# Turned probabilities kept in landing order, and the row scatters spread out, in a two-layer gated attention and expert kernel

## The reference

```
# cross attention: 16 heads, 8 key/value heads, 128 context tokens of width 128
q = (layernorm(x) @ Wq);  k = ctx @ Wk;  v = ctx @ Wv
attn = softmax(where(mask, q k^T / sqrt(128), -inf))
x = x + tanh(g) * ((attn v) @ Wo)
# 8 experts, each token takes 2; a shared expert beside them
logits = x @ W_router.T;  rw, sel = top_k(softmax(logits), 2)
x = x + tanh(g) * (shared(x) * sigmoid(x @ W_sgate.T) + sum of rw * expert_sel(x))
```

## Time and profile before

| | us |
|---|---|
| median of 3 runs (1302.22 to 1304.45) | 1303.56 |
| the profiled execution | 1302.48 |
| its span in the profile | 1300.7 |
| mean granted clock of TensorE | 0.989 |
| busy: PE, DVE, ACT, POOL | 1240.1, 894.9, 738.5, 549.1 |
| the next stage begins (first product with `ws`) | 1108.56 |

### The profile page before, as it was taken

One profiled execution on the slowest core, in us unless ns is written; L12 is line 12 of the kernel. 1 busy time (PEld: TensorE's weight loads), 2 busy tenths in 40 slices (PEclk: granted clock), 3 DMA queues, 4 the chain that ended last, 5 costly groups with the idle time before them and its releaser, 6 DMA issues. The chain is left out here.

```text
span 1300.7 us, 23370 instructions
## 1 busy us (share of the span) xinstructions
PE 1240.1 (95%) x7907; PEld 1098.9 (84%) x7907; DVE 894.9 (69%) x2453; ACT 738.5 (57%) x2053; POOL 549.1 (42%) x542
## 2 busy tenths in 40 slices
PE   6899999999999989999999989999999988999998
PEld 4788888888888878888888888899988977888987
DVE  6678788887988776743433346657687776788857
ACT  4777787777877743322222247666565653546542
POOL 3564456644565533200000001866668675223430
PEclk9999999999999989999999999999999998999999
DMA  7000000000000310398100011434343355413434
GB/s 266 10 1 1 9 1 1 1 9 0 0 0 1 74 31 2 113 326 245 64 0 1 1 18 49 142 112 136 100 138 130 115 179 166 118 45 99 129 100 174
DMA packets 85672, 101.09 MB, mean 78 GB/s; under 512 B 16985, under 2 KB 72802, under 8 KB 85186
## 3 DMA queue, kind: packets, MB, share of 16 engines
q1 hardware_dynamic: 82162, 90.45, 23.1%
q0 software_dynamic: 3408, 9.34, 2.0%
HBM read 53.60 MB, written 46.18 MB: 77 GB/s over the span
## 5 line engine op out<-in xcount | busy, mean ns | idle before, releaser
L98 PE MATMUL bank<-wvo_hi,pc_hi_a 128*128 128x256 f32 x512 | 149.7, 292 | 6.5 <-DVE pc_lo_a L1337 5.7
L1748 ACT ACTIVATE act_g_f<-bank 128x512 f32<-128x512 f32 x64 | 38.2, 598 | 190.9 <-PE bank L100 190.9
L100 PE MATMUL bank<-wvo_hi,pc_lo_a 128*128 128x256 f32 x512 | 144.8, 283 | 0.0
L99 PE MATMUL bank<-wvo_lo,pc_hi_a 128*128 128x256 f32 x512 | 144.6, 283 | 0.0
L1807 DVE TENSOR_TENSOR hid_f<-act_g_f,bank 128x512 f32<-128x512 f32 x64 | 44.0, 688 | 142.3 <-ACT act_g_f L1748 142.3
L877 ACT ACTIVATE probs_a<-bank,nbias_a,q_r_a 128x128 f32<-128x128 f32 x256 | 114.4, 472 | 23.7 <-DVE nbias_a L995 23.4
L140 POOL TENSOR_TENSOR rstd<-mv,half 128x4 f32<-128x4 f32 x12 | 12.2, 1020 | 260.7 <-DVE mv L135 260.7
L1055 POOL TENSOR_TENSOR probs_a<-probs_a,rden_a 128x512 f32<-128x512 f32 x64 | 66.6, 1041 | 103.8 <-DVE rden_a L1001 103.8
L98 PEld LDWEIGHTS bank<-wvo_hi,pc_hi_a 128*128 128x128 f32 x512 | 98.2, 192 | 12.5 <-DVE pc_lo_a L1337 8.3
L1277 ACT ACTIVATE probs_a<-probs_a,nmin_a 128x128 f32<-128x128 f32 x256 | 99.5, 392 | 7.7 <-DVE nmin_a L1321 7.4
L99 PEld LDWEIGHTS bank<-wvo_lo,pc_hi_a 128*128 128x128 f32 x512 | 98.5, 192 | 3.2
(11 more groups left out here) (314 smaller groups left out, 4139.9 us busy)
## 6 DMA issues: line engine op xcount, KB each, us to landing
rows_in<-blank_f SPq DMA_DIRECT2D x8, 2193.0 KB, 21.1
staged<-blocks_a SPq DMA_DIRECT2D x32, 512.0 KB, 2.9
turned_a<-staged SPq DMA_DIRECT2D x128, 128.0 KB, 2.9
xs_raw_f<-rows_in SPq DMA_DIRECT2D x39, 129.0 KB
y_tok_f<-rows_out SPq DMA_DIRECT2D x4, 1024.0 KB, 8.9
we_raw<-in_L_ffn_We_gate_up SPq DMA_DIRECT2D x2, 1408.0 KB, 9.9
ctx_raw_a<-in_ctx SPq DMA_DIRECT2D x8, 256.0 KB, 3.0
x_sb<-in_x SPq DMA_DIRECT2D x4, 512.0 KB, 10.1
```

Of the source, the lines that this page charges most:

```text
L98: nc.tensor.matmul(out, w[0], x[0], start=start, stop=False)
L99: nc.tensor.matmul(out, w[0], x[1], start=False, stop=False)
L100: return nc.tensor.matmul(out, w[1], x[0], start=False, stop=stop)
```

## The change

Four things, all in the second attention and the router. `pt` keeps the order in which the turned probabilities land (block, head, token); the context product then gives its columns in that order, and `Ch` and `Cl` read the bank and write `pc` through views that put heads and tokens right. A step `SC` issues one scatter, for one slot, so that a group has eight steps: group 0's at s = 35 to 42 (it had four of two scatters at 35 to 38), group 1's at 51, 52, 53 and 58 to 62 (51 to 54). Group 2's routing moves ahead by up to two iterations: NA from s = 52 to 50, the moments and root from 53 to 51, NX from 56 to 54, RT from 57 to 56, RQ from 60 to 58, PL from 63 to 61. The last transpose, unit 63's, moves from the start of v = 64 to the end of v = 63.

```diff
@@ second_order
-               30: "RQ0", 32: "RQ1", 33: "RK0", 34: "PL0 PL1", 35: "SC0", 36: "SC1", 37: "SC2", 38: "SC3"}
-    hurried = {15: "E0", 17: "E1", 20: "NA0 NA1", 21: "NA2 NA3 NM0", 22: "NB0 NB1", 23: "NB2 NB3", 24: "NX0 NX1", 25: "RT0 RL0", 26: "RS0",
-               28: "RQ0", 29: "RQ1", 30: "RK0", 31: "PL0 PL1"}
+               30: "RQ0", 32: "RQ1", 33: "RK0", 34: "PL0 PL1"}
+    scatter = [{35 + n: f"SC{n}" for n in range(8)}, {51: "SC0", 52: "SC1", 53: "SC2", 58: "SC3", 59: "SC4", 60: "SC5", 61: "SC6", 62: "SC7"}]
+    hurried = {15: "E0", 17: "E1", 18: "NA0 NA1", 19: "NA2 NA3 NM0", 20: "NB0 NB1", 21: "NB2 NB3", 22: "NX0 NX1", 24: "RT0 RL0", 25: "RS0",
+               26: "RQ0", 27: "RQ1", 28: "RK0", 29: "PL0 PL1"}
...
-        unit(v - 1, "TV")
+        if v < U:
+            unit(v - 1, "TV")
...
+        for r in range(2):
+            words(scatter[r].get(s, ""), r)
         unit(s, "Ch", "Cl")
...
+        if v == U - 1:
+            unit(v, "TV")
         words(following.get(s, ""))
@@ second_attention
+        def by_block(v):
+            return v.rearrange("p h (i t) -> p i h t", i=4)
...
-                    nc.scalar.activation(flat(pc[0][:, n % 2, :, :]), c_bank[n % 2][:, :], ACT.Copy).then_inc(sem("pc_hi_ready"), 1)
+                    nc.scalar.activation(by_block(pc[0][:, n % 2, :, :]), c_bank[n % 2][:, :].rearrange("p (i h t) -> p i h t", i=4, h=QH), ACT.Copy).then_inc(sem("pc_hi_ready"), 1)
...
-                    hi, lo = (flat(v[:, n % 2, :, :]) for v in pc)
-                    nc.vector.tensor_tensor(lo, c_bank[n % 2][:, :], f32(hi), ALU.subtract).then_inc(sem("pc_ready"), 1)
+                    hi, lo = (by_block(v[:, n % 2, :, :]) for v in pc)
+                    nc.vector.tensor_tensor(lo, c_bank[n % 2][:, :].rearrange("p (i h t) -> p i h t", i=4, h=QH), f32(hi), ALU.subtract).then_inc(sem("pc_ready"), 1)
...
-                    nc.gpsimd.tensor_copy(pt[0][:, n % 2, :].rearrange("p (h i t) -> p i h t", h=QH, i=4),
-                                          turned[:, n // 2 % 2, :, n % 2, :].rearrange("p i (h t) -> p i h t", h=QH)).then_inc(sem("pt_hi_ready"), 1)
+                    nc.gpsimd.tensor_copy(pt[0][:, n % 2, :].rearrange("p (i x) -> p i x", i=4), turned[:, n // 2 % 2, :, n % 2, :]).then_inc(sem("pt_hi_ready"), 1)
...
-                    hi, lo = (v[:, n % 2, :].rearrange("p (h i t) -> p i h t", h=QH, i=4) for v in pt)
-                    nc.gpsimd.tensor_tensor(lo, turned[:, n // 2 % 2, :, n % 2, :].rearrange("p i (h t) -> p i h t", h=QH), f32(hi),
-                                            ALU.subtract).then_inc(sem("pt_ready"), 1)
+                    hi, lo = (v[:, n % 2, :].rearrange("p (i x) -> p i x", i=4) for v in pt)
+                    nc.gpsimd.tensor_tensor(lo, turned[:, n // 2 % 2, :, n % 2, :], f32(hi), ALU.subtract).then_inc(sem("pt_ready"), 1)
@@ Router.gpsimd_step
-            b = m * GB + i
+            b, r = m * GB + i // 2, i % 2
             pool.wait_ge(self.places_ready, m + 1)
-            for r in range(2):
-                self.scatter(self.pay[:, b, :], self.row_of[:, r, b:b + 1], self.rows_in[:, :], self.rows_sent)
+            self.scatter(self.pay[:, b, :], self.row_of[:, r, b:b + 1], self.rows_in[:, :], self.rows_sent)
@@ routed_feed_forward, extras: the same scatters, in the same places, as eight steps a group
-        0: [..., "SC 2 0", "SC 2 1", "SC 2 2", "SC 2 3"],
+        0: [..., *(f"SC 2 {n}" for n in range(8))],
-        7: ["PL 3 0", "PL 3 1", "SC 3 0", "SC 3 1", "SC 3 2", "SC 3 3", "SE 4"],
+        7: ["PL 3 0", "PL 3 1", *(f"SC 3 {n}" for n in range(8)), "SE 4"],
```

More of the change, by code:

```diff
@@ L2136, in routed_feed_forward @@
     extras = {
[1 row of a table removed]
+        0: ["NB 3 0", "NB 3 1", "NB 3 2", "NB 3 3", *(f"SC 2 {n}" for n in range(8))],
         1: ["X 1 0", "X 1 1", "SD 0", "SD 1", "SD 2"],
```

## The result

The changed kernel takes 1292.7 us at the median of 6 runs (1290.94 to 1293.85), the kernel before 1303.46 (1302.22 to 1304.87) in 6 beside them: a ratio of 0.9915, with a 95% interval of 0.9902 to 0.9928. It is faster, by 10.8, which is under 1%. The profiled execution took 1293.64, with a span of 1291.9. Both kernels run 23370 instructions; TensorE is busy for 1238.0 against 1240.1.

What follows compares the result with a forecast made beforehand. TensorE bounds steady slices; elsewhere it waits for GpSimd, slowed by scatter pairs, and VectorE. 1.8 + 8.7 + 1.6 - 1.6 = 10.5, rounded down to 10.2, gave 1292.3 profiled, 1293.4 median; range 1290 to 1299.5.

Steps and rivals of the forecast that it cites:

- Bound and places: Second attention: TensorE sets the pace, falling short where scatters go out, at 999.64 (1.82) and units 54 to 56 (7.2).
- Landing order, nothing: GpSimd's copy and subtraction, context bank readers: simpler or permuted views bring no gain and no loss.
- The slower rival: VectorE's permuted low halves rise by 1.0 to 1.7, making the kernel 8 slower, 1311.6; chance 0.05.
- Group 0, 1.8: Group 0's scatters, s = 35 to 42: one per iteration removes TensorE's wait at 999.64, 1.8 gained.
- (a): Group 2's root at s = 51: GpSimd waits for VectorE's moments, unit 53's copy 2.4 later, TensorE waits 1.3 to 1.4.
- (b): GpSimd's queue up to unit 57's subtraction, fewer scatters ahead: unit 57's context product starts earlier, 5.4 gained.
- the rival of an early fall: Stalls at units 51 to 54 halve TensorE's clock from unit 54; gain only 4.7, 1298.9; chance 0.18.
- (c): Unit 57's product to its low half: ScalarE's context copies are freed of token copies and most router delay, 3.2 gained.
- The tail, nothing: Units 57 to 63, paced by VectorE: 20.0 instead of 21.6, the 1.6 cancelled by 1.6 allowed for half clock.
- The rival in which scatters hold VectorE up by 3.3: Tail: five scatters each delay VectorE by 0.65, 3.3 lost, gain 6.9, 1296.7; chance 0.14.
- The one in which nothing reaches the end: VectorE's fixed queue sets the tail, so only group 0's 1.8 or less is gained, 1301.8; chance 0.06.
- The rule weighed there: VectorE two-input or two-port instructions and GpSimd's exclude each other; earlier trace agreed for copies, showed no wait for scatters.

Runs made afterwards that it cites:

- run 23370: Not a follow-up run: both kernels, the changed one and the one before, run 23370 instructions.
- The second profile: The changed kernel once more, unaltered, profiled a second time and timed in 5 runs: 1291.67 us, ratio 0.9905.

## Why the prediction was right, and where its sizes were off

**Bound and places: held.** Both stretches with a wait for GpSimd's low half were set by pairs of scatters: put the pairs back, and each wait is back (1.89 at unit 40; with the routing late as before, 1.54, 3.29 and 1.51 at units 54 to 56, where the kernel before had 1.58, 3.21 and 2.42).

**Landing order, nothing: held.** Subtraction 1290 ns against a forecast near 1290, low half 690; undone, the same. The slower rival needed a low half of 1.5, and fell.

**Group 0, 1.8: undersized.** It measured 2.4. I priced the wait as it is listed; the product that waits came 2.36 late.

**(a) The root's wait: held.** Counted from unit 50's product (1047.24 in the trace of before, 1046.69 now), I had the moments at 7.8 and unit 53's copy at 10.0; they came at 7.7 and 10.0 (1054.37 and 1056.70). The waits at units 53 and 54 were 1.23 and 0.89, for 1.3 to 1.4 each. What the walk had not asked is what stands behind this wait: VectorE's low half, nearly as late.

**(b) Unit 57's product, 5.4: held.** 32.60 to 27.20 is 5.4; the product was to come 27.16 behind unit 50's, at the full clock that was assumed. The granted clock from 1050 to 1075 shows 1.00, and 0.47 to 0.50 for each product up to unit 57's says the same, so the rival of an early fall did not come.

**(c) The tokens' and router's copies ahead of the low half, 3.2: oversized.** It gave 2.1. The mechanism is there (the low half came 5.01 after its product, not 7.14), but I gave VectorE's sums 0.84 and laid everything end to end; two of their operations alone, on 4 elements each, took 0.48 and 1.08 beside GpSimd's copy and subtraction. The second profile has 4.55 for this stretch (1072.88 to 1077.43), a gain of 2.6, so part of the miss is the spread of a single profile.

**The tail, nothing: the number held, 0.4, and part of that is luck.** I had a stretch shorter by 1.6 and 1.6 of half clock against it. The second profile, at a full clock throughout, needed 19.95 from unit 57's low half to the next stage, which is the 20.0 of the walk: a gain of 1.6. In the first the clock was indeed at half around unit 58 (0.89 over the slice from 1065), but that isn't what ate the gain. With the landing order undone the clock was at half there too (0.66 from 1075 to 1080), and the stretch took 19.96. The 1.2 lay in VectorE's queue, 18.24 against 17.02. And the walk let that queue set the pace to its end, while it does so only to unit 59's low half; behind it TensorE is busy for all of the last 10.74. Nor did I see unit 58's wait of 2.90 for its transfer. The rival in which scatters hold VectorE up by 3.3 falls with the run that took them out: stage 282.54 against 282.25 and 280.62. The one in which nothing reaches the end falls with the stage, 10.4 shorter. The last transpose, costed at nothing, is not settled: 1.4 and 3.0 in the stage, nothing in the median.

**The rule weighed there: it held for copies, and not for scatters.** Small operations of VectorE that start beside a subtraction of GpSimd's end with it. GpSimd's timeline of the changed kernel:

```profile
1077.47 1.27 POOL L1381 TENSOR_TENSOR pt_lo_a<-turned_a,pt_hi_a 128x512 fp32r<-128x512 f32 x1
...
1087.16 1.27 POOL L1381 TENSOR_TENSOR pt_lo_a<-turned_a,pt_hi_a 128x512 fp32r<-128x512 f32 x1
```

and VectorE's, of an operation on 32 elements a partition:

```profile
1087.19 1.27 DVE L2026 TENSOR_SCALAR chosen_r<-rank_r 128x32 f32<-128x32 f32 x1
1088.38 0.17 DVE L2027 TENSOR_SCALAR chosen_r<-rank_r 128x32 f32<-128x32 f32 x1
```

The same kind of operation takes 0.17 right behind; the long one ends at 1088.46, the subtraction at 1088.43. The gates' 1.08 at 1077.69 ends at 1078.77, the subtraction at 1078.74. In the run without scatters in the tail L2026 falls elsewhere and takes 0.17. VectorE's low half, which reads one of its inputs from a bank, is not held up: twelve of them that start beside a subtraction take 0.67 to 0.69, as the others do. That is the rule of the Trainium skill, "SBUF — State Buffer", "Who interferes with whom", by which the later of two such instructions waits; the trace agrees, if VectorE runs these one-input operations in the two-port mode that the rule asks for, which no row shows. Taking the five scatters away shortened nothing, as the trace of before had it.

**The sum.** 2.4 + 5.4 + 2.1 + 0.4 is 10.4 in the stage (10.37 before each term is rounded); 10.5 was forecast, rounded down to 10.2. The two errors in size, 0.6 and -1.1, and the tail's 0.4 nearly cancel. That the match is so close is luck: the second profile has 12.0, with 2.6 and 1.6 for the last two terms, which the range of the forecast holds too. The medians differ by 10.8, the two profiled executions by 8.8, since the code before the stage, which is the same, came out 1.9 longer in the second.

**What was not seen.** I had the routing's shift as part of one gain of 8.7, its loss in (a) and its gain in (c), and never summed it by itself. It pays only because it pulls the router out of the last seven units and the ranking ahead in them: 1.7 lost ahead of unit 57, 4.5 to 6.1 won behind it. And the gain of (b) took the half clock between units 56 and 57 in without a price of its own; it was 2.6 of the 5.4.

## What to carry to other kernels

Work that an engine does for somebody else belongs one item to an iteration, above all where iteration plus item just fits under the pace of the engine that sets it: here 4.2 fits under 4.34, and 5.45 doesn't. The items that don't fit can go where another engine sets the pace, as five scatters did in the tail. Before work is moved out of a tail, find the last wait of the engine that ends it: what stood behind that wait gained nothing here by moving. When work is moved ahead, look for what waits on the way in its new place as well as for what it frees in the old one; and before a wait is filled, ask which engine would be waited for next, since it may stand a few tenths behind. Measure landmarks from the first one of the stage, in two profiles of the same kernel, before explaining a microsecond of its tail.

## What the runs showed that I had not expected

- TensorE's clock falls in one profile and not in another of the same kernel: after the router's 16 products and a wait of 1.5 for VectorE's low half, the first had 0.67 from 1075 to 1080, the second 1.00. The profile with the landing order undone had 0.66 there as well, and yet a stage of 280.54: the clock alone doesn't make the 1.6.
- The kernel before and the one with both parts of group 1's change undone reach unit 56's product within 0.1 of each other, behind waits of 2.42 and 1.51, and from there one has half its clock until about 1080 and the other all of it: 2.6 of difference that no wait shows, since TensorE is busy.
- An operation of VectorE on 4 elements a partition lasts until what it meets on GpSimd is done: one of the router's sums (L2006) took 0.15, 0.21, 0.38, 0.48, 1.16, 1.23 and 1.27 in seven of these kernels' profiles. The 1.23, without scatters in the tail, ends at 1077.25, GpSimd's subtraction at 1077.22.
- In group 1's pairs the second scatter shows 0.96 to 0.97 with 0.30 to 0.31 of idle time ahead, the first 1.02 to 1.07 with 0.15 to 0.20: either way it keeps GpSimd's queue for 1.2 to 1.3.
